# New orders for all five engines and new PSUM banks in the layered part of a transformer with experts

## The reference

```python
x = x + cross_attention_L0(ctx, layernorm(x), cond)       # 16 heads of 64
x = x + bit_linear_ffn(layernorm(x))                       # weights in {-1, 0, 1}, hidden 512
y = layernorm(x)
for i in range(6):                                         # the layered part
    n = ln(y) * (1 + g1[i]) + b1[i]                        # g, b: cond @ n1_w[i].T + n1_b[i]
    q, k, v = rope(...), rope(...), ...                    # from n @ qkv_w[i].T, 16 heads of 8
    y = y + softmax(q k^T / sqrt(8)) v @ so_w[i].T
    n = ln(y) * (1 + g2[i]) + b2[i]
    y = y + cross_attention(rope(n @ cq_w[i].T), 77 context tokens) @ co_w[i].T
    n = ln(y) * (1 + g3[i]) + b3[i]
    y = y + gelu(n @ f1_w[i].T + f1_b[i]) @ f2_w[i].T + f2_b[i]      # hidden 512
x = x + y
x = x + experts(x)                                         # top 1 of 8, hidden 64
```

## Time and profile before

| | |
|---|---|
| time, median of 3 runs | 2361.25 us (2357.6 to 2362.25) |
| span of the profiled execution | 2365.3 us (the profile gives no other time of its own) |
| busy: PE, DVE, ACT, POOL | 2218.9 (94%), 1930.4 (82%), 1761.9 (74%), 1082.6 (46%) us |
| f2 of the first, second and third step | starts at 836.6, 904.1, 972.0 us |
| f2 of the last three steps | starts at 2230.9, 2278.0, 2315.6 us |
| maximum 0 of the first three steps | starts at 617.9, 678.8, 743.0 us |
| weigh 15 of the last step | at 2229.7 us |

### The profile page before, as it was taken

The page is one execution under the profiler, slowest core; times in us unless marked ns, Lnnn a source line. Parts: engine busy times, 40 slices in busy tenths (PEclk is TensorE's granted clock), DMA queues, the critical chain, the costliest instruction groups (busy, mean ns, idle before and its releaser), DMA issues.

```text
span 2365.3 us, 46233 instructions
## 1 busy us (share of the span) xinstructions
PE 2218.9 (94%) x17034; PEld 960.1 (41%) x17034; DVE 1930.4 (82%) x3983; ACT 1761.9 (74%) x3601; POOL 1082.6 (46%) x1348
## 2 busy tenths in 40 slices
PE   6999999999688999999999999999999999999979
PEld 3455455545322333333343333333343334333336
DVE  6778889698778888888888888898888888888435
ACT  4778778696166778788888787887888887777744
POOL 3656556466334434434444443533454444432324
PEclk9999999999589999999999999999999999999979
DMA  2000000000312211212222321212222322111000
GB/s 84 2 1 1 1 2 1 30 1 20 90 50 63 82 50 54 65 46 72 62 67 69 82 63 48 67 51 66 54 74 63 81 63 66 49 49 52 25 23 19
DMA packets 108570, 113.07 MB, mean 48 GB/s; under 512 B 15809, under 2 KB 96951, under 8 KB 107319
## 3 DMA queue, kind: packets, MB, share of 16 engines
q1 hardware_dynamic: 108345, 110.12, 17.1%
HBM read 14.80 MB, written 1.05 MB: 7 GB/s over the span
## 4 chain that ended last, share of the span: by engine, by line
PE 63%; DVE 14%; ACT 10%; DMA 4%; POOL 4%; issue 3%; SPq 2%; DVEq 0%; POOLq 0%; ACTq 0%
PE psum L1487 11%; PE psum L1455 6%; PE psum L1467 6%; DVE A L1977 5%; PE psum L1258 4%; PE psum L1599 4%; PE psum L1591 4%; PE psum L1559 3%; PE psum L1388 3%; PE psum L1342 3%; DMA A<-A 3%; ACT A L2137 3%; DVE A L1999 3%; PE psum L1548 2%; PE psum L1354 2%
## 5 line engine op out<-in xcount | busy, mean ns | idle before, releaser
L1977 DVE TENSOR_REDUCE A<-psum 128x1 f32<-128x512 f32 x1536 | 969.9, 682 | 141.5 <-PE psum L1467 133.4
L2197 ACT ACTIVATE A<-psum 128x512 f32<-128x512 f32 x1536 | 821.4, 604 | 206.0 <-PE psum L1455 177.9
L1467 PE MATMUL psum<-A 64*128 64x512 bf16 x1536 | 421.8, 391 | 35.9 <-DVE A L1977 12.8
L1455 PE MATMUL psum<-A 64*128 64x512 bf16 x1536 | 403.9, 384 | 15.6 <-DVE A L1977 6.0
L1487 PE MATMUL psum<-A 128*9 128x512 f32 (+1 forms) x3072 | 405.2, 604 | 1.6 <-ACT A L2197 1.5
L2342 POOL TENSOR_TENSOR A<-A,rden 128x512 f32<-128x512 f32 x256 | 266.7, 1067 | 177.5 <-DVE rden L1862 176.7
L2373 POOL TENSOR_TENSOR A<-A 128x512 f32<-128x512 f32 (+1 forms) x78 | 96.6, 1239 | 301.8 <-DMA A<-A 291.8
L1467 PEld LDWEIGHTS psum<-A 64*128 64x128 bf16 x1536 | 105.1, 94 | 309.7 <-DVE A L1977 116.7
L2227 ACT ACTIVATE A<-psum 77x512 f32<-77x512 f32 x384 | 199.7, 598 | 30.3 <-PE psum L1548 29.7
L1455 PEld LDWEIGHTS psum<-A 64*128 64x128 bf16 x1536 | 103.5, 94 | 277.2 <-DVE A L1977 103.8
L2137 ACT ACTIVATE A<-psum,nm 128x512 f32<-128x512 f32 x256 | 176.0, 688 | 45.0 <-DVE nm L1850 44.1
(11 more groups left out here) (209 smaller groups left out, 3743.4 us busy)
## 6 DMA issues: line engine op xcount, KB each, us to landing
A<-A SPq DMA_DIRECT2D x456, 128.0 KB, 2.4
A<-A SPq DMA_DIRECT2D x336, 64.0 KB, 2.0
A<-zero SPq DMA_DIRECT2D x51, 128.0 KB, 2.4
wl<-in_wl SPq DMA_DIRECT2D x6, 1024.0 KB, 5.8
A<-A SPq DMA_DIRECT2D x36, 78.0 KB, 2.1
A<-in_nT SPq DMA_DIRECT2D x1, 1664.0 KB, 6.8
A<-in_w SPq DMA_DIRECT2D x2, 512.0 KB, 7.0
A<-in_w SPq DMA_DIRECT2D x1, 1024.0 KB, 6.1
```

The lines of the kernel that those rows point to most:

```text
L1455: handle.matmul(bank(b), k_st[bt][lo:lo + ROW, h // 2, k * P:(k + 1) * P], q_st[m % 3][lo:lo + ROW, h // 2, :], start=True, stop=True).the ...
L1467: handle.matmul(bank(b), q_st[m % 3][lo:lo + ROW, pair, q * P:(q + 1) * P], k_st[bt][lo:lo + ROW, pair, :], start=True, stop=True).then_in ...
L1977: handle.tensor_reduce(nm[:, pair // 4, q, j, pair % 4:pair % 4 + 1], bank(BANKS["maximum"][i]), AX.X, ALU.max, negate=True).then_inc(mx, 1)
L2197: handle.activation(pT[:, block % 2, i % GROUP, :], bank(BANKS["scores"][i]), ACT.Exp, scale=HD1 ** -0.5).then_inc(ex, 1)
```

## The change

Nothing is computed otherwise and no part is added or left out: both kernels have 4796 parts of PE, 2335 of ACT, 2215 of DVE, 295 of POOL and 339 of SP in the layered walk and its guests. New are the values in `TENSOR`, `SCALAR`, `VECTOR`, `POOL`, `SYNC`; 22 of the 24 entries of `BANKS` (all but `f2` and `weigh`); and the guests: `PLACED_TENSOR` has 291 places for 270, `PLACED_SCALAR` 86 for 54, `PLACED_VECTOR` 81 for 69, `PLACED_POOL` 15 for 12, `PLACED_SYNC` 3 for 13. The tables of the first phase and the banks of the experts are only written with another indent. Two waits are new in the code.

```diff
         TENSOR = {
...
-            "maximum": [427, 429, 434, 436, 437, 442, 445, 446, 448, 450, 453, 456, 458, 460, 462, 463, 472, 473, 476, 479, 481, 483,
...
-            "c_turn": 825,
-            "shift_turn": [524, 632],
-            "cq": 832,
...
-            "cross_max": [884, 912, 924, 925, 931, 938, 947, 956],
...
-            "f1": [1099, 1102, 1103, 1104],
-            "f2": 1110,
-            "s_turn": 364,
-            "qk": [369, 380],
-            "cshift_turn": 966,
...
-            "v": 382,
...
+                        "maximum": [461, 462, 463, 466, 468, 472, 473, 475, 477, 479, 484, 487, 492, 493, 495, 498, 502, 503,
...
+                        "qk": [397, 412],
...
+                        "v": 450,
...
+                        "shift_turn": [548, 667],
+                        "c_turn": 865,
...
+                        "cq": 882,
...
+                        "cross_max": [934, 939, 950, 958, 967, 969, 970, 973],
+                        "f1": [1132, 1133, 1137, 1138],
+                        "f2": 1144,
+                        "s_turn": 384,
+                        "cshift_turn": 981,
...
         VECTOR = {
...
-            "x_so": 91,
...
-            "cross_max": [132, 145, 151, 152, 155, 159, 164, 167],
-            "x_f": 237,
...
-            "qk_rope": [-101, -100, -96, -95],
...
+                        "cross_max": [140, 143, 148, 151, 155, 156, 157, 158],
+                        "x_f": 237,
...
+                        "qk_rope": [-104, -103, -96, -95],
+                        "x_so": 82,
...
         PLACED_TENSOR = {
-            ("qk", 0, 0): [("condition", 0, None)],
-            ("v", 0, 0): [("condition", 1, None), ("condition", 2, None)],
-            ("maximum", 0, 0): [("condition", 3, None)],
-            ("maximum", 11, 0): [("b_turn", 0, None)],
-            ("maximum", 16, 0): [("b_up", 0, None)],
-            ("maximum", 22, 0): [("b_up", 1, None)],
...
-            ("cshift_turn", 0, 22): [("f2", 0, 21)],
...
-            ("cross_scores", 0, 23): [("f2", 0, 22)],
...
+                        ("qk", 0, 0): [("v", 0, 0)],
+                        ("maximum", 2, 0): [("condition", 0, None), ("condition", 1, None)],
+                        ("maximum", 9, 0): [("condition", 2, None), ("b_turn", 0, None)],
+                        ("maximum", 13, 0): [("b_up", 0, None), ("b_up", 1, None)],
+                        ("maximum", 17, 0): [("condition", 3, None)],
...
+                        ("weigh", 14, 23): [("f2", 0, 21)],
...
+                        ("f2", 0, 22): [("cross_max", 2, 23)],
...
+                        ("f2", 0, 23): [("e_up", 0, 21), ("e_logits", 0, 21), ("e_turn2", 2, 20), ("e_turn2", 3, 20)],
...
         BANKS = {
...
-            "shift_turn": [7, 2],
...
-            "f1": [1, 2, 6, 0],
...
-            "cross_max": [[6, 7], [3, 4], [6, 7], [2, 3], [3, 4], [3, 4], [6, 7], [3, 4]],
...
+                        "shift_turn": [7, 3],
...
+                        "f1": [6, 4, 7, 0],
...
+                        "cross_max": [[1, 2], [2, 3], [1, 2], [2, 3], [0, 1], [3, 4], [1, 2], [4, 5]],
...
+            summed = {}
+
             def moments(src, st, mv, n, rows):
+                dve.wait_ge(d_own, summed.get(id(st), 0))
                 for q in range(n):
                     t = handle.bn_stats(st[0:rows, q, :], src[0:rows, q, :])
                 t.then_inc(own.next(), 1)
...
                 for q in range(n):
                     t = handle.bn_aggr(mv[0:rows, q, :], st[0:rows, q, :])
                 t.then_inc(own.next(), 1)
+                summed[id(st)] = own.n
                 after_own()
 
             def variance(src, chain, n, rows):
...
                     block = 16 * m + i // GROUP
                     act.wait_ge(sc_ps, 64 * m + i + 1)
                     act.wait_ge(pv_ps, block - 1)
+                    if i == GROUP and m == 0:
+                        act.wait_ge(zeroed, 18 * 16)
                     handle.activation(pT[:, block % 2, i % GROUP, :], bank(BANKS["scores"][i]), ACT.Exp, scale=HD1 ** -0.5).then_inc(ex, 1)
                 if name == "shift_out":
                     act.wait_ge(sh_ps, 2 * m + i + 1)
```

More of the change, by code:

```diff
@@ L742, in build @@
-            ("cross_scores", 10, 21): [("maximum", 58, 23), ("maximum", 59, 23), ("weigh", 4, 23)],
-            ("scores", 24, 23): [("scores", 23, 23)],
-            ("scores", 26, 23): [("cross_scores", 11, 21), ("scores", 25, 23)],
-            ("maximum", 63, 23): [("maximum", 62, 23)],
-            ("weigh", 5, 23): [("scores", 27, 23)],
-            ("cross_scores", 13, 21): [("c_turn", 0, 22), ("cross_scores", 12, 21)],
-            ("co_turn", 0, 21): [("cross_scores", 14, 21)],
-            ("scores", 29, 23): [("cross_weigh", 2, 21), ("shift_turn", 1, 23)],
@@ L750, in build @@
-            ("cross_weigh", 3, 21): [("cross_scores", 15, 21), ("cq", 0, 22), ("weigh", 6, 23)],
-            ("co_turn", 1, 21): [("scores", 35, 23)],
-            ("scores", 38, 23): [("catt_turn", 0, 21)],
-            ("scores", 44, 23): [("scores", 43, 23)],
-            ("scores", 48, 23): [("o_turn", 0, 23)],
-            ("scores", 49, 23): [("weigh", 10, 23)],
-            ("scores", 53, 23): [("cross_max", 0, 22)],
-            ("scores", 54, 23): [("f_turn", 0, 21)],
-            ("f1", 0, 21): [("cross_max", 1, 22)],
@@ new lines, in build @@
+                        ("maximum", 37, 0): [("s_turn", 0, 1)],
+                        ("maximum", 39, 0): [("scores", 4, 0), ("weigh", 0, 0)],
+                        ("scores", 6, 0): [("qk", 0, 1)],
+                        ("maximum", 42, 0): [("scores", 7, 0)],
+                        ("scores", 10, 0): [("weigh", 1, 0), ("maximum", 45, 0)],
+                        ("maximum", 48, 0): [("scores", 11, 0)],
+                        ("scores", 13, 0): [("maximum", 49, 0), ("maximum", 50, 0), ("scores", 12, 0)],
@@ new lines, in build @@
+                        ("scores", 30, 0): [("weigh", 5, 0), ("weigh", 6, 0)],
+                        ("maximum", 3, 1): [("scores", 31, 0)],
+                        ("shift_turn", 1, 0): [("maximum", 5, 1)],
+                        ("maximum", 6, 1): [("weigh", 7, 0), ("b_turn2", 0, None), ("b_turn2", 1, None), ("ck", 0, 0),
+                ("scores", 32, 0)],
+                        ("scores", 33, 0): [("b_down", 0, None)],
+                        ("maximum", 10, 1): [("scores", 34, 0)],
+                        ("scores", 36, 0): [("maximum", 12, 1)],
+                        ("o_turn", 0, 0): [("scores", 40, 0)],
+                        ("maximum", 16, 1): [("weigh", 9, 0), ("scores", 41, 0), ("scores", 42, 0), ("scores", 43, 0),
@@ new lines, in build @@
+                        ("x_so", 0, 2): [("max", 49, 3)],
+                        ("max", 57, 3): [("c_stats", 0, 2)],
+                        ("cdivide", 0, 1): [("max", 63, 3)],
+                        ("max", 33, 4): [("x_f", 0, 1)],
+                        ("cross_max", 3, 2): [("cross_max", 2, 2), ("max", 36, 4)],
+                        ("max", 37, 4): [("cross_max", 4, 2)],
+                        ("cdivide", 0, 2): [("max", 63, 4)],
+                        ("max", 15, 5): [("cdivide", 1, 2)],
@@ new lines, in build @@
+                        ("cdivide", 0, 21): [("max", 63, 23)],
+                        ("cross_max", 4, 22): [("x_f", 0, 21)],
+                        ("x_so", 0, 23): [("ck_rope", 0, 23), ("ck_rope", 1, 23), ("e_stats", 0, 20), ("e_norm", 0, 20)],
+                        ("cq_rope", 0, 23): [("e_stats", 0, 21)],
+                        ("cdivide", 1, 22): [("cdivide", 0, 22)],
+                        ("x_f", 0, 22): [("cross_max", 2, 23)],
+                        ("cdivide", 0, 23): [("e_norm", 0, 21), ("e_top", 0, 20), ("e_stats", 0, 22)],
```

1274 lines of the change are left out of this document (666 added, 608 removed), and 6 rows, old and new, of the table PLACED_POOL.

## The result

The changed kernel takes 2378.07 us in the median of 4 runs (2374.06 to 2379.8), the kernel before 2361.75 in 4: ratio 1.006, 95% interval 1.0039 to 1.008. It is 0.6% slower. I had forecast 2354.7 us, 6.5 us faster; the time lies outside my range of 2340 to 2370, and on the other side.

The account below looks back on a forecast made before the run. PE was taken to set the pace, with short waits on other engines, the largest behind f2. Start +11.5, second step -1, inner steps -15, end -2 gave -6.5 us: 2354.7 us against a median of 2361.25, range 2340 to 2370.

Parts of the forecast that it names:

- The steady part: Layered steps, third step to weigh 15 of the last: 15 us faster, a plain step 63.9 us for 65.2.
- Slots and bank sums: PE work counted by matmul slots, plus deficits where a bank's reader takes longer than PE's work between: 257.6 for 262.4 us.
- my sum up to weigh 15: Step-by-step differences from the third step, together -21, with +8 for the last stretch; put down as -15 us.
- DVE would hardly wait for f2 at x_f: Sign in the new profile: DVE's wait for f2 in x_f near nothing instead of 46.5 us.
- The beginning: First step: late condition piece delays other_rows, shift_rows and scores 0; +11.5 us, bounds +5 to +14.
- the last piece: Last group of condition matmuls on PE, now behind maximum 16: to end at about 634 (630 to 636), before at 611.7.
- the hole: PE idle before scores 0 of the first step; no further clock loss charged, some 2 us by the rule.
- Rival A: The hole at the start closes: +2 in place of +11.5, 2345 us; chance 0.22.
- The second step: Its windows are 55.4 to 55.7; with the warmer start, 1 us faster.
- Rival B: Rope, swap DMA, POOL and row DMAs up to the next maximum 0 set the step: 2366.8 us; chance 0.20.
- C: New bank clashes at cross_max 4 to 7: 1.9 us more a step, near 2390, or 2373 us; chance 0.08.
- The end: From weigh 15 of the last step to the end, 132.8 us before: 2 us faster, bounds -6 to +3.

Follow-up runs that it names:

- control: The changed kernel run once more, unaltered, beside its variants: 2377.68 us, ratio 1.0055 to the kernel before.
- xf1: Changed kernel with x_f and max 34 exchanged on DVE, x_f one place earlier in each step: 2406.06 us, ratio 1.0174 to the kernel before.
- bank5: Changed kernel with cross_max 5 in banks 2 and 3 instead of 3 and 4: 2395.9 us, ratio 1.013 to the kernel before.
- late_before2: Second run of the kernel before with its last condition piece moved from ahead of maximum 0 to ahead of maximum 17: 2379.88 us, ratio 1.0061.
- cond_early: Changed kernel with all four condition guests ahead of maximum 0 on PE, gains 4 right behind gains 3 on ACT: 2360.28 us, ratio 0.9987.
- both: Changed kernel with the edits of cond_early and tail together: 2354.61 us, ratio 0.9963 to the kernel before.
- tail2: Version both with expert work (up 0, logits, turns 2 and 3) moved behind f2 of the last step: 2361.11 us, ratio 0.9983 to the kernel before.
- f21: Version both with f2 of step 21 ahead of cshift_turn of step 22, its x_f behind the last step's divide: 2354.68 us, ratio 0.996.
- tail: Changed kernel with cross_max 3 to 7 and cshift_turn of the last step ahead of f2 of step 22: 2373.03 us, ratio 1.0044.
- best: Version both with the f2 move of f21 and gains 1 and 2 ahead of b_scale on ACT: 2349.56 us, ratio 0.9933.

## Why the prediction was wrong

*The steady part was right.* Slots and bank sums gave 257.6 for 262.4 us in four steps. From f2 to f2 the traces have 259.5 for 262.7; over the steps 9 to 20 one takes 64.62 us for 65.79 from maximum 0 to maximum 0, so 4.7 us less in four for the 4.8 that I had. That it comes so near is in part luck: the control has 64.97, 3.3 us less in four. (In my sum up to weigh 15, -21 and +8 give -13, not the -15 that I put down.) Behind f2 PE now has one wait of 0.35 us where the earlier trace rows have 0.68, 0.39 and 0.32:

```profile
1563.58 3.84 PE L1672 MATMUL psum<-wl,A 128*128 128x128 f32 x32
...
1574.76 0.32 PE L1604 MATMUL psum<-A 64*128 64x77 bf16 x8 [0.35 <-DVE A L2076]
```

The waits of PE from 1000 to 1900 us (in total, times, longest), before:

```profile
PE psum L1531 <- ACT A L2197: 9.5, 14, 0.7
PE psum L1531 <- DVE A L1977: 5.1, 13, 0.4
PE psum L1467 <- DVE A L1999: 4.2, 13, 0.3
```

and in the changed kernel:

```profile
PE psum L1604 <- DVE A L2076: 4.9, 14, 0.4
```

That is 1.4 us a step before and 0.35 now: these waits account for 1.0 us of the steady gain. One reading of them was wrong. I had put all three down to DVE's queue; the largest, 0.68 us in each step, ends with an `exp` on ACT.

xf1 and bank5 changed one place and one bank and lost 1.45 and 0.75 us a step against the first trace of the changed kernel, 1.26 and 0.57 against the control, where the sums said 1.28 and 0.58: right in sign, place and size. That DVE would hardly wait for f2 at x_f was wrong, and the sum didn't need it: it waits 60.0 us in 23 waits for 46.5 in 19. What counts is how little PE asks of DVE just behind it.

*The beginning: right chain, wrong price.* The step that failed is "two pieces 3.4, ... a piece 2.4, ... the last piece 2.4 ...: it ends at about 634". These are near the price of the first pieces before, of which 40 matmuls ran in 5.43 us from 600.3 on at a mean clock of 0.81, while the last piece of the earlier trace rows shows 3.98 us for 18 already, and the sentence ahead of the sum says that the clock is 0.50. At half the clock 28 of them take 6.13 us and 20 take 4.43: 6.13 - 3.4 + 2 x (4.43 - 2.4) = 6.8 us, and the end came 6.3 us late (640.3 for 634). other_rows took what I had said (23.4 for 23.5), and shift_rows 3.1 us for 2.2. From scores 0 on another 2.5 us are lost up to maximum 0 of the second step, at a clock of 0.73 where the kernel before has 0.88 in the same stretch.

I had weighed a rule for that. "TensorE: Matmul & The Clock Gate" of the Trainium skill, section "HAM oscillation", says that idle gaps send the array back to the half clock, and it restarts cold. By it the hole would have cost some 2 us, which I had not charged. The versions do not bear out that the hole causes this loss. With the old orders the stretch takes 30.9 us at 0.88 without the hole (the kernel before) and 31.0 at 0.88 with it (late_before2). With the new orders the control has the hole, cond_early has none, and the control is the shorter one (first the control, then cond_early):

```profile
668.90:699.90 31.00, 24.33 (x117) 6.04 (x117) 26.79 (x51) 17.86 (x33) 15.43 (x13) 0.84 0.25 68
650.20:683.60 33.40, 27.16 (x117) 6.42 (x117) 27.34 (x52) 17.72 (x32) 15.90 (x16) 0.73 0.23 64
```

Over all versions of the changed kernel the stretch takes 30.3 to 31.0 us at a clock of 0.84 to 0.91 in some traces (control, bank5, both, tail2, f21) and 33.3 to 33.6 at 0.73 in others (changed, tail, xf1, cond_early, best), with and without the hole in either group. What decides it is open.

cond_early and late_before2 show the late piece by itself: 17.4 us back, and 13 us lost by a like move in the kernel before.

*Rival A* (the hole closes) is refuted: late_before2 is 12.9 us late at the second step and 13.4 at the end.

*The second step* gives 6.8 us, not 1. It does so in cond_early too and not in late_before2, so it comes from the new orders at a point where the clock is part of it: 1.00 in the changed kernel, 0.92 before. My estimate of the most that the clock can be is 0.08 of 64.2 us, 5.1 us; how much is clock and how much order is open.

*Rival B* (the rope chain sets the step) is refuted: behind the beginning `maximum` waits for no more than 1.1 us of DMA in all. *C* had a clash of cross_max 4 to 7 at 1.9 us; it is 0.35 us for one of them. (Its 2373 goes with half of the 38 us, not with a quarter.)

*The end: -2 said, +9.4 measured.* The step that failed is "The 3.85 us of f2 leave it ... against that ... cross_scores of the last step stands directly behind f2 of step 22 (+3.5 exposed)": I counted parts that leave and enter, and not what waits. By the table in the section on the result, f2 of step 21 left the way from weigh 15 to cross_max 0, and it takes 34.9 us as before; PE waits for the rows of cross_max 0 at its end (4.35 us for 3.29). And f2 of step 22 stood directly ahead of cross_scores 0 before the change, where it covered a wait; it stands ahead of cross_max 3 now. That costs 6.4 us up to cshift_turn and gives back 0.8 behind it. The other 4.1 us are lost between cross_scores 0 and the last f2, where the clock is 0.76 for 0.80, f_turn waits 1.69 us for POOL, and three turns of the experts stand that stood behind f2. Which of these costs how much is open.

Putting cross_max 3 to 7 in front gave 3 us of the end stretch and 4.6 of the time, and left 5.6 us between cross_scores 0 and the last f2 (in both, from -16.5 to -10.9 against the kernel before). Two candidates for these are out: moving expert work behind the last f2 shortens the way to it by 2.6 us and lengthens the rest by 7.7 (tail2), and f2 of step 21 changes nothing in the time that can be told (f21). An expert product now stands ahead of co_turn 1 and one behind it, and turns of the experts ahead of f_turn; moving these wasn't tried.

In the traces I was 13 us off (+6.5 for -6.5): 9.9 by the late piece at half clock and what follows it, 11.4 by the end, less 5.8 by the second step and 2.5 by the steady part. In the medians it is 23 (2378.1 for 2354.7); the other 10 lie between single executions and medians. I had set a difference of stretches of one execution, some 6 us above its median and not 4, against that median, and the changed kernel's execution is 4 us below its own.

## What to carry to other kernels

Price a matmul that you move by the clock at the place where it lands: 48 matmuls of `condition` take 5.42 us at a granted clock of 1.00 (cond_early, 2.3 us for 20), and 20 take 4.43 us at 0.50. Before moving a small part that "has time", follow its semaphore into the other engines' queues and count the time it has: here a piece of 4 us released 23 us of DMA issues on an in-order queue, the next matmuls stood behind these, and of 22.5 us of delay only 10.6 were free. When a part leaves a stretch, ask whether it covered a wait there. And a steady gain of 1.0 to 1.2 us a step, real and predictable from the work between a bank's reader and its next writer, is worth less than the two ends of the program if these are laid out anew along with it.

## What the runs showed that I had not expected

The bank sums are sharp: exchanging two neighbours on DVE cost 28 us of 2378 by one wait of 1.15 us a step. The 15 DMA issues of other_rows, with the wait for the zeros among them, took 23.4 to 23.7 us in every trace read, whether the queue had been idle before them (the changed kernel) or not (the kernel before); the five with zeros take 7.4 to 7.9 us of it in all of them. And two executions of one kernel can differ by 2.3 us in a stretch of 33 (changed and control), so a term of that size needs more than one trace.
